# One decoder layer on one core: every engine's written-out order of steps replaced by another

## The reference

```
q, k, v = x @ Wqkv.T                    # 16 heads of 8; q, k = elu + 1
kv = sum_n k[n] v[n];  out = q kv / (q sum_n k[n]);  x += out @ Wproj.T + bproj     # "self"
scores = q k.T / sqrt(8), causal; softmax; x += (softmax @ v) @ Wo.T                # "cross", k and v from ctx
top 2 of 8 experts by sigmoid(x @ Wr); 4 experts are gated MLPs, 2 scale x, 1 is relu; + causal conv of 4 taps   # "ffn"
```

## Time and profile before

| | |
|---|---|
| median of 3 runs | 183.39 us (183.13 to 184.17) |
| profiled execution, its own time | 183.81 us |
| its span, first to last instruction | 182.1 us |
| busy share of the span | PE 91%, DVE 87%, ACT 70%, POOL 65% |
| mean granted TensorE clock | 0.989 of full speed |

### The profile page before, as it was taken

The page is one execution under the profiler, slowest core; times in us unless marked ns, Lnnn a source line. Parts: engine busy times, 40 slices in busy tenths (PEclk is TensorE's granted clock), DMA queues, the critical chain, the costliest instruction groups (busy, mean ns, idle before and its releaser), DMA issues.

```text
span 182.1 us, 5254 instructions
## 1 busy us (share of the span) xinstructions
PE 166.1 (91%) x1856; PEld 115.9 (64%) x1856; DVE 157.5 (87%) x448; ACT 127.5 (70%) x289; POOL 118.8 (65%) x248
## 2 busy tenths in 40 slices
...
## 3 DMA queue, kind: packets, MB, share of 16 engines
...
...
HBM read 3.10 MB, written 1.05 MB: 23 GB/s over the span
## 4 chain that ended last, share of the span: by engine, by line
PE 53%; DVE 14%; POOL 12%; issue 9%; ACT 6%; DMA 3%; SPq 2%; POOLq 0%; DVEq 0%
PE pv_bank L871 11%; PE max_pair L871 10%; PE soft_pair L871 8%; PE ffn_bank L871 8%; PE self_bank L871 5%; PE cross_bank L871 4%; DVE negmax L761 4%; POOL probs L523 3%; POOL rstd L497 3%; ACT xn L570 2%; SPq L385 2%; DMA ks<-kparts 2%; DVE conv L849 1%; PE ffn_bank L875 1%; PE cross_bank L875 1%
## 5 line engine op out<-in xcount | busy, mean ns | idle before, releaser
L761 DVE TENSOR_REDUCE negmax<-max_pair 128x4 f32<-128x1024 f32 (+1 forms) x48 | 58.5, 1218 | 7.1 <-PE max_pair L871 6.6
L627 ACT ACTIVATE probs<-soft_pair 128x1024 f32<-128x1024 f32 x48 | 49.3, 1026 | 11.1 <-PE soft_pair L871 10.5
L523 POOL TENSOR_SCALAR_AFFINE_SELECT probs<-probs 128x512 f32<-128x512 f32 (+1 forms) x48 | 37.9, 801 | 17.3 <-ACT probs L627 16.5
L871 PE MATMUL pv_bank<-probs,vs 128*32 128x256 f32 (+1 forms) x448 | 21.1, 329 | 0.0
L871 PE MATMUL soft_pair<-qs,ks 64*128 64x256 bf16 (+1 forms) x256 | 18.8, 246 | 0.5 <-issue 0.4
L871 PE MATMUL max_pair<-ks,qs 64*128 64x128 bf16 (+1 forms) x256 | 18.5, 242 | 0.0
L497 POOL TENSOR_TENSOR rstd<-vareps,exponent 128x2 f32<-128x2 f32 x24 | 17.1, 712 | 2.0
L871 PE MATMUL max_pair<-causal,picks 64*128 64x128 bf16 (+1 forms) x192 | 15.3, 237 | 3.4 <-issue 1.2
L871 PEld LDWEIGHTS pv_bank<-probs,vs 128*32 128x32 f32 x448 | 12.8, 109 | 7.1 <-issue 1.7
L570 ACT ACTIVATE xn<-inputs,shift,rstd 128x128 f32<-128x128 f32 x32 | 14.0, 502 | 3.0 <-POOL shift L499 3.0
L871 PE MATMUL ffn_bank<-inputs,x3T 128*128 128x8 f32 (+1 forms) x46 | 15.5, 433 | 0.0
...
## 6 DMA issues: line engine op xcount, KB each, us to landing
...
qs<-maxparts SPq DMA_DIRECT2D x32, 4.0 KB
...
```

The source lines that it names most:

```text
L523: nc.gpsimd.affine_select(out=v, in_=v, compare_op=ALU.is_ge, fill=0.0, base=0, pattern=[[0, n], [1, P]], channel_multiplier=-1).then_inc( ...
L627: nc.scalar.activation(probs[b.par][g][:, k, :], soft_pair[:, :], ACT.Exp).then_inc(exp_done, 1)
L761: nc.vector.tensor_reduce(maxima, max_pair[:, :].rearrange("p (u h k) -> p u h k", u=2, h=n), AX.X, ALU.max, negate=True).then_inc(max_rea ...
L871: return nc.tensor.matmul(out, lhsT, rhs, start=start, stop=stop, skip_group_check=True)
```

## The change

All five lists of `ORDER` are replaced. The steps in them are the same, with one exception on PE: three warm steps (2, 2 and 1 matmuls, all near the end) become `warm.0.5` near the start and two warm steps of 2 near the end. The position in the list changes for 69 of 84 steps on SP, 87 of 147 on POOL, 142 of 232 on ACT, 249 of 360 on DVE and 240 of 291 on PE, mostly by a few places. Outside the lists three waits change:

```diff
@@ zero_max
                 if b.since(4):
-                    sp.wait_ge(pe_soft, b.count(UNITS, -3 * UNITS))
@@ normalise
-                    if b.since(2):
-                        if n == 3:
-                            act.wait_ge(relu7_done, b.count(2, -2))
@@ residual2
                 dve.wait_ge(pe_o, b.count(1, 1))
+                if b.since(2):
+                    dve.wait_ge(skip_done, b.count(2, -2))
@@ "pe", first row of the table
-        self_x_t.0.0 self_q1.0.0 cross_k.0.0 self_kv.0.0 self_x_t.1.0 cross_v.0.0 self_sum.0.0 self_q1.1.0 self_x_t.2.0
+        self_x_t.0.0 self_q1.0.0 warm.0.5 self_kv.0.0 cross_k.0.0 self_x_t.1.0 self_sum.0.0 self_x_t.2.0 self_out.0.0
```

More of the change, by code:

```diff
@@ L31 @@
     "sp": """
[L32 to L40, removed]
+        load.0.0 load.0.1 load.0.2 load.0.6 load.0.3 load.0.4 load.0.5 load.0.7 hi_k.0.0 mid_k.0.0 lo_k.0.0 hi_q.0.0
+        mid_q.0.0 lo_q.0.0 hi_k.1.0 mid_k.1.0 lo_k.1.0 hi_q.1.0 mid_q.1.0 lo_q.1.0 send_max.0.0 send_max.0.1 hi_k.2.0
@@ new lines @@
+        hi_q.2.0 mid_q.2.0 lo_q.2.0 hi_q.3.0 mid_q.3.0 mid_k.2.0 lo_k.2.0 send_max.1.0 lo_q.3.0 send_max.1.1 hi_k.3.0
+        mid_k.3.0 lo_k.3.0 send_max.2.0 zero_max.4.0 hi_k.4.0 mid_k.4.0 lo_k.4.0 hi_k.5.0 send_max.2.1 mid_k.5.0
+        hi_q.4.0 zero_max.5.0 lo_k.5.0 mid_q.4.0 send_max.3.0 lo_q.4.0 hi_q.5.0 hi_k.6.0 send_max.3.1 send_max.4.0
+        store_out.0.0 mid_q.5.0 lo_q.5.0 hi_q.6.0 mid_q.6.0 lo_q.6.0 send_max.4.1 mid_k.6.0 lo_k.6.0 hi_k.7.0
+        store_out.1.0 send_max.5.0 zero_max.6.0 zero_max.7.0 mid_k.7.0 lo_k.7.0 hi_q.7.0 mid_q.7.0 send_max.5.1 lo_q.7.0
@@ L46 @@
[L46 to L55, removed]
+        causal.0.0 heads.0.0 rstd1.0.0 rstd1.1.0 ones.0.0 picks.0.0 ones.0.1 rstd1.2.0 rstd1.3.0 bias.0.0 clear_v.0.0
@@ L61 @@
[L61 to L65, removed]
@@ new lines @@
+        tap.1.0 div2.2.1 route.1.0 reduce.4.4 route.1.1 gate.1.0 times_up.1.0 route.1.2 reduce.4.5 rest_q.6.0 route.1.3
+        tap.1.1 x2.2.0 route.1.4 reduce.5.0 route.1.5 max_mid.4.1 gate.1.1 route.1.6 times_up.1.1 route.1.7 reduce.5.1
+        tap.1.2 stats3.2.0 skip.1.0 var3.2.0 reduce.5.2 skip.1.1 rest_k.7.0 div2.3.0 reduce.5.3 finish.1.0 div2.3.1
+        max_mid.5.0 reduce.5.4 tap.2.0 tap.2.1 reduce.5.5 tap.2.2 route.2.0 route.2.1 x2.3.0 gate.2.0 route.2.2
+        reduce.6.0 times_up.2.0 route.2.3 max_mid.5.1 route.2.4 reduce.6.1 route.2.5 route.2.6 rest_q.7.0 route.2.7
```

163 lines of the change are left out of this document (87 added, 76 removed).

## The result

The changed kernel takes 189.75 us in the median of 6 runs (187.63 to 192.18), against 183.79 us (183.13 to 185.09) for the kernel before in the same session. The ratio is 1.028, with a 95% interval from 1.021 to 1.035: 6 us slower by the medians (5.1 by the ratio), and outside the predicted range of 181.8 to 186.4. The profiled execution took 190.49 us, its span 188.8 us. Its mean granted clock was 0.973; in the six runs it lay between 0.973 and 0.991, and the fastest run is the one with 0.991.

What follows compares the result with a forecast made beforehand. PE was taken as nearly full, with SP's copy queue deciding where it stops. Terms −0.6 + 1.2 − 1.2 + 1.5 − 0.2 + 0 + 0.7, less 0.3, gave +1.1 us: 184.5 us, range 181.8 to 186.4.

Steps and rivals of the forecast that it cites:

- Batch 3 (−1.2): Ahead of `max.3.0`: `lo_q.3` now lands before PE wants it, so PE's 1.21 us wait goes away, −1.2 us.
- Batch 4 (+1.5): Ahead of `max.4.0`: `lo_q.4` goes out later in SP's queue and PE stalls, +1.5 us (0.5 to 3).
- Batch 2 (+1.2): Ahead of `max.2.0`: `lo_k.2` stands behind 16 operand DMAs on SP and PE stalls, +1.2 us (1.0 to 3.1).
- The clock: TensorE's granted clock, falling near the start after PE's idle times: left as it is in the sum.
- The start (−0.6): Up to `max.0.0`: reordered steps on PE, ACT and POOL bring it earlier, −0.6 us (0 to −1.0).
- The tail (+0.7): From `x2.7.0` to the end on DVE: `tap.6.0` and `route.6.0` now come later, +0.7 us (0 to +1.0).
- Absorption (−0.3): Whole kernel: ACT and POOL catch up during a stall and later small waits shrink, −0.3 us.
- The rivals with copies in time: Batches 2 and 4: one stall absent, 183.0 to 183.3 us (chance 0.20); both absent, 181.8 us (0.15).
- the one with the clock: Rival: TensorE stays at 2.4 GHz through the first 15 us, total 183.0 us; chance 0.12.
- The blocking of DVE and POOL: Rival: three more tail taps run beside a POOL step, adding 1.5 us, total 186.0 us; chance 0.08.

## Why the prediction was wrong

*Batch 3 (−1.2)* came out as written, with 0.14 us of wait left. *Batch 4 (+1.5)* came out at 1.50, and that is partly luck. `lo_q.4` was issued at 88.88 us, 4.2 later than the 84.7 of the sum, but PE wanted `max.4.0` at 89.77, 4.8 later than its 84.98. In the other kernels with the same SP list at this place the wait was 1.44, 2.06 and 2.15 us.

*Batch 2 (+1.2)* is the term whose size failed, with 2.27 us in its place. The mechanism is confirmed two ways: moved away, and put into the other kernel. The landing was forecast for 58.6 us and came at 60.25: `send_max.0.1` began at 45.43 us, 0.74 later than `max_mid.0.1` of before allowed, and `hi_q.3` took 1.34 us longer to issue than the 1.86 in the earlier trace rows. The range of 1.0 to 3.1 for this term held it. The 0.66 us of PE's steps that now stand between `max.0.0` and `max.1.0` were not in the sum at all, and they are also why `max_mid.0.1` was late: the count took its time from the old order.

*The clock* is the step that failed the forecast most. "In the sum I leave the clock as it is" was argued for the start alone, and the clock of the middle and the tail was put at nothing without a reason. That a wait of PE of 2 us in the middle can itself lower the clock was not asked, although show a fall behind idle times of 1.74 and 0.32 us. It costs some 1.4 us behind `max.2.0` and 1.3 in the tail. The sum treated each wait as a term of its own, and they are not independent of the clock. Of the 5.6 us by which the profiled execution exceeds the forecast's +1.1, the clock is 2.7, batch 2 with PE's moved steps 1.7, the start 0.55, and the 0.35 ahead of `max.4.0` together with the absorption that did not come 0.65.

*The start (−0.6)* brought −0.05. `self_kv.0` starts at 12.46 instead of 10.75 us, behind the warm step's 2.34 us, and up to `max.0.0` this is made up for, in part because `self_out.4` and `self_x_t.6` no longer stand ahead of it. Whether the warm step is a loss or a gain differs between the two bases (a gain of 0.4 to 0.8 us on the changed order, where the intervals overlap; a loss of about 1.2 us by the ratios on that of before, where they don't), and why stays open.

*The tail (+0.7)* was right in its order's part: 0.6 us where the clock stayed up, 0.4 of them DVE's. *Absorption (−0.3)* did not come; apart from `max.5.0`'s own wait nothing caught up. Between `max.5.0` and `x2.7.0` the delay stayed at 4.7 us for 60 us; with PE busy for 90% of the span nothing absorbed it.

The rivals with copies in time did not come; the one with the clock had the right subject and the wrong sign. The blocking of DVE and POOL did not come either: the 24 taps took 520 ns in the mean (median 476) with their new neighbours, and 544 (median 480) before.
